# Normalising attention probabilities: one product over four heads instead of two products over two heads each

## The chip, the cores and the metric

The kernel runs on one core of one Trainium2 chip. The metric is the device time of one execution in microseconds. In the profile, PE is TensorE's matmul, PEld its weight load, DVE is VectorE, ACT ScalarE, POOL GpSimd and SP SyncE.

## What is computed

The reference takes x of 8 sequences x 512 tokens x 128 channels and applies three residual steps, each to a layer-normalised input: half of a mixture of experts (8 experts, the best 2 per token, hidden size 512, exact GELU), attention, and half of the same mixture again. The attention has 16 heads of 64 channels, but keys and values are shared by all heads:

```python
q = (x @ Wq).reshape(B, N, h, dh).transpose(0, 2, 1, 3) * scale
kv = x @ Wkv
k, v = (kv[..., :dh], kv[..., dh:])
sim = jnp.einsum('bhid,bjd->bhij', q, k) + bias
sim = jnp.where(causal, -max, sim)
attn = jax.nn.softmax(sim, axis=-1)
out = jnp.einsum('bhij,bjd->bhid', attn, v)
out = out.transpose(0, 2, 1, 3).reshape(B, N, h * dh) @ Wout + bout
```

What matters here is the softmax: each row of exponentials is multiplied by the reciprocal of its sum.

## The kernel before

Everything is in tiles of 128 tokens; there are 32. The kernel has three stages one behind the other: the first mixture of experts (`ffn_*(0)`, 78 expert tiles), attention, and the second mixture (`ffn_*(1)`, 71 expert tiles). Beside the attention, further work of the two mixtures is spread: on POOL the gathers of the first mixture's result (task GA, L757, an indirect DMA for each of two choices of a token tile), on VectorE the combining of it (CB, L1225 and L1230), layer-norm statistics (L974 to L996) and deviations (L1003 to L1007), the scaled rows of the next layer norm (LN, L1243, and X2, L1165), the second routing (H2, L1179 to L1190; W3, L1193 to L1195; B2, L1202 to L1217), and at last the scatter of the rows to their experts (SC, L775, on POOL again).

Attention goes through 8 sequences b, in each through 16 units n = 4g + t: a group g of four heads and a query tile t. Because of the causal mask a unit has (t + 1) x 128 key columns for each head. The steps of one unit are:

- S (TensorE, L1496): scores of four heads in banks.
- TTR (VectorE, L1268), one for each head: adds the bias, writes the negated scores to `prob` and the minimum to `negmax`.
- EXP (ScalarE, L935), one for each head: the exponential in place, with its sum in `lsum`.
- R (VectorE, L1275): the reciprocals of four sums, in `rsum`.
- N (POOL, L785): multiplies `prob` by `rsum`, in place, in two instructions of two heads each.
- T (TensorE, L1505): transposes, four for each key tile; the first waits for N (L1503).
- TC (VectorE, L1281, or ScalarE, L942): copies four transposes from their bank to `pT`.
- AV (TensorE, L1521), O (ScalarE, L948), Y (TensorE, L1528), YA (VectorE, L1290): product with the values, its copy, the output projection and its sum into `x_sb`.

`prob` has 8 buffers, so S of a unit waits for the last T of the unit 8 before. No loop fixes the order in which an engine issues these tasks. A planner (`attention_order`, L453 to L515) runs over a table of tasks, each with a cost in microseconds for the engine that does it and the tasks that it needs (`attention_tasks`, L321); it gives each engine, whenever it is free, that ready task which is wanted earliest (`wanted_at`, L413), and reserves banks as it goes. Its answer, one list for each engine, is the program order. An engine works through its own list strictly in order. The numbers that semaphores are waited for are counted from these lists (`counted`, L521).

The two places that say what a normalisation costs and how it is counted, and the two instructions:

```python
task(("N", b, n), {"pool": (1.25, 2.1, 2.95, 3.8)[t]}, [("R", b, n)])          # L365
NORM, BOUT = counted("pool", ("N",), 2), counted("pool", ("BO",))              # L537
```

Of the kernel before, what the change touches and what calls it, by code (L numbers as in the profile page):

```python
# [9 lines left out]
P = 128  # L10
# [16 lines left out]
HG, NG = 4, 4  # L27
QT = SEQ // P
# [26 lines left out]
ALU = mybir.AluOpType  # L55
# [25 lines left out]
def build(nc, x, Wq, Wkv, Wout, bout, rel_emb, gate_w, fc_w, proj_w, out):  # L81
    ctx = ExitStack()
    with ctx:
# [107 lines left out]
        with att:  # L191
# [11 lines left out]
            prob = [ab(f"prob{n}", [P, HG, (n % QT + 1) * P]) for n in range(8)]  # L203
            negmax = ab("negmax", [P, 8])
            lsum = ab("lsum", [P, 8, HG])
            rsum = ab("rsum", [P, 8, HG])
# [110 lines left out]
        def product_of(t, c):  # L317

            return 0 if t < 2 else c

        def attention_tasks():  # L321
# [3 lines left out]
            def task(name, cost, needs, takes=None, frees=None, banks=1):  # L325
                tasks[name] = (cost, needs, takes and (takes, banks), frees if frees is None or type(frees[0]) is tuple else (frees, 0))

            for b in range(BATCH):
                for q in range(QT):
                    task(("GA", b, q), {"pool": 2.6}, [("CB", b - 1, q // 2)])  # L330
                for z in range(2):
                    opened = [("QL", 0, 0, 1), ("KL", 0)] if b == 1 else []
                    task(("CB", b, z), {"dve": 1.6}, [("GA", b, 2 * z), ("GA", b, 2 * z + 1)] + opened)
                task(("LS", b), {"dve": 2.6}, [("CB", b, 0), ("CB", b, 1), ("LN", b - 1)])
                task(("LA", b), {"act": 3.4}, [("LS", b)])
                task(("LN", b), {"dve": 2.0}, [("xT", b - 1), ("LA", b)])
                task(("BO", b), {"pool": 1.3}, [("LN", b)] + ([("KL", 0)] if b == 0 else []))
                task(("xT", b), {"pe": 0.45}, [("LN", b), ("Q", b - 2, NG - 1, 1), ("V", b - 2), ("K", b - 2)] +
                     ([("N", 0, QT)] if b == 1 else []), "front")
                task(("xTh", b), {"act": 0.48}, [("xT", b), ("Q", b - 2, NG - 1, 1), ("V", b - 2), ("K", b - 2)])  # L340
                task(("xTl", b), {"dve": 0.6}, [("xTh", b)], None, ("xT", b))
                task(("K", b), {"pe": 0.7}, [("xTl", b)] + [("S", b - 2, NU - 1, c) for c in range(2)], "front")
                task(("KH", b), {"act": 0.48}, [("K", b)] + [("S", b - 2, NU - 1, c) for c in range(2)])
                task(("KL", b), {"dve": 0.6}, [("KH", b)], None, ("K", b))
                task(("V", b), {"pe": 1.1}, [("xTl", b), ("AV", b - 2, NU - 1)], "front")
                task(("VC", b), {"act": 0.3}, [("V", b), ("AV", b - 2, NU - 1)], None, ("V", b))
                for g in range(NG):
                    for c in range(2):
                        b2, g2 = (b, g - 2) if g >= 2 else (b - 1, g - 2 + NG)
                        task(("Q", b, g, c), {"pe": 0.7}, [("xTl", b), ("S", b2, g2 * QT + QT - 1, c)], "front")  # L350
                        task(("QH", b, g, c), {"act": 0.5}, [("Q", b, g, c), ("S", b2, g2 * QT + QT - 1, c)])
                        task(("QL", b, g, c), {"dve": 0.6}, [("QH", b, g, c)], None, ("Q", b, g, c))
                for n in range(NU):
                    g, t = divmod(n, QT)
                    for pairs in products(t):
                        task(("S", b, n, pairs[0]), {"pe": (0.68, 0.68, 0.5, 0.66)[t]},
                             [("KL", b), ("T", *earlier(b, n, 8), t)] + [("QL", b, g, c) for c in pairs], "front", None, 2)
                    for h in range(HG):
                        s_task = ("S", b, n, product_of(t, h // 2))
                        others = [("TTR", b, n, h - 2)] if len(products(t)) == 1 and h >= 2 else []  # L360
                        task(("TTR", b, n, h), {"dve": (0.28, 0.41, 0.55, 0.68)[t]}, [s_task, ("EXP", *earlier(b, n, 2), h)] + others,
                             None, (s_task, h % 2) if others or len(products(t)) == 2 else None)
                        task(("EXP", b, n, h), {"act": (0.385, 0.49, 0.6, 0.71)[t]}, [("TTR", b, n, h), ("R", *earlier(b, n, 8))])
                    task(("R", b, n), {"dve": 0.12}, [("EXP", b, n, h) for h in range(HG)] + [("N", *earlier(b, n, 8))])
                    task(("N", b, n), {"pool": (1.25, 2.1, 2.95, 3.8)[t]}, [("R", b, n)])  # L365
                    for jj in range(t + 1):
                        task(("T", b, n, jj), {"pe": 0.44}, [("N", b, n)], "turned")
                        task(("TC", b, n, jj), {"act": 0.48, "dve": 0.6}, [("T", b, n, jj), ("AV", *ring_user(b, n, jj))],
                             None, ("T", b, n, jj))
                    task(("AV", b, n), {"pe": 0.43 * (t + 1) + 0.05}, [("TC", b, n, jj) for jj in range(t + 1)] +  # L370
                         ([("VC", b)] if n == 0 else []) + [("YA", *earlier(b, n, 2))])
                    task(("O", b, n), {"act": 0.36}, [("AV", b, n), ("Y", *earlier(b, n, 2))])
                    task(("Y", b, n), {"pe": 0.45}, [("O", b, n)])
                    task(("YA", b, n), {"dve": 0.25}, [("Y", b, n), ("BO", b)])
                for q in range(QT):
                    task(("ST", b * QT + q), {"dve": 0.25}, [("YA", b, NU - QT + q)])
# [157 lines left out]
        PT_ACT, PT_DVE = counted("act", ("TC",)), counted("dve", ("TC",))  # L534
        MISC_FREE, S_DONE, RSUM = counted("dve", ("xTl", "KL", "QL")), counted("dve", ("TTR",)), counted("dve", ("R",))
        XA_DONE, PROJ_DONE = counted("dve", ("LN",), QT), counted("dve", ("YA",))
        NORM, BOUT = counted("pool", ("N",), 2), counted("pool", ("BO",))  # L537
        YG_DONE = counted("dve", ("CB",), 2)
        XN2_DONE = counted("dve", ("X2",))
        XNT2_PS, XNT2_SB, LOGIT2_PS, LOGIT2_SB = counted("pe", ("T2",)), counted("act", ("C2",)), counted("pe", ("L2",)), counted("dve", ("G2",))  # L540
# [155 lines left out]
        def _(gp):  # L696
            g = nc.gpsimd
# [50 lines left out]
            def attention_pool(tasks):  # L748
                for k in tasks:
                    kind, b = k[0], k[1]  # L750
                    if kind == "GA":
                        q = k[2]
                        t = b * QT + q
                        if b >= 1:
                            gp.wait_ge(yg_done, YG_DONE["CB", b - 1, q // 2])
                        for c in range(TOPK):
                            g.indirect_dma_start(out=yg[:, q, c, :], out_offset=None, in_=y1_dram[t // HT],  # L757
                                                 in_offset=bass.IndirectOffsetOnAxis(ap=pos_row[:, c * TILES + t:c * TILES + t + 1], axis=0),
                                                 ).then_inc(yg_in[q], 16)
                    elif kind == "BO":  # L760

                        gp.wait_ge(xa_done, XA_DONE["LN", b])
                        xb = x_sb[:, b * QT:(b + 1) * QT, :]
                        g.tensor_tensor(out=xb, in0=xb, in1=bout_sb[:].unsqueeze(1).to_broadcast([P, QT, D]),
                                        op=ALU.add).then_inc(bout_done, 1)
                    elif kind == "SC":
                        t = k[1]
                        gp.wait_ge(pos2_done, group_of(t) + 1)
                        gp.wait_ge(id_done, group_of(t) + 1)
                        gp.wait_ge(weights_done, 3 + group_of(t))  # L770
                        if t == 0:
                            gp.wait_ge(fill_done, 16 * FILLS)
                        j = t % (2 * QT)
                        for c in range(TOPK):
                            g.indirect_dma_start(out=slot_dram, in_=slot[:, j, :], in_offset=None,  # L775
                                                 out_offset=bass.IndirectOffsetOnAxis(ap=idx2[:, c, j:j + 1], axis=0),
                                                 ).then_inc(slot_out[half(t)], 16)
                    elif kind == "N":
                        _, _, n = k

                        gp.wait_ge(rsum_done, RSUM["R", b, n])
                        for c in range(2):
                            hs = slice(2 * c, 2 * c + 2)
                            pv = prob[n % 8][:, hs, :]
                            g.tensor_tensor(out=pv, in0=pv, in1=rsum[:, n % 8, hs].unsqueeze(2).to_broadcast([P, 2, (n % QT + 1) * P]),  # L785
                                            op=ALU.mult).then_inc(norm_done, 1)

            def ffn_pool(r):
                k0 = START[r]
# [815 lines left out]
```

## Time and profile before

| | |
|---|---|
| median of 3 runs | 1073.82 us (1072.75 to 1073.89) |
| the profiled execution, its own time | 1075.41 us |
| its span, first to last instruction | 1073.6 us |
| mean granted TensorE clock | 0.962 |
| busy in the span: PE, DVE, ACT, POOL | 950.6, 823.8, 630.6, 621.4 us |
| attention, first normalisation to last projection | 221.6 to about 886 us |

The profiled execution took 1.6 us more than the median of the runs, and 1.8 us more than its span. Busy time says how long an engine had an instruction under way, also one that stood waiting for a shared resource inside itself; a wait for a semaphore counts as idle. A sum over the whole span mixes the three stages, so the attention stage is read by itself below.

### The profile page before, as it was taken

To read this page: it belongs to the slowest core of one execution; us is meant where nothing else is said; L and a number is where in the kernel's file an instruction comes from. 1 tells how busy PE (TensorE), PEld (TensorE's weight loads), DVE (VectorE), ACT (ScalarE), POOL (GpSimd) and SP (SyncE) were. 2 spreads that over 40 slices of the span, in tenths; PEclk is the share of its full clock that TensorE was granted. 3 is DMA by queue.
4 is the path that set the end of the run, shared out by engine and by line. 5 is a ranking of instruction groups with operands and counts; after the bars stand their busy time and mean duration, and the time that the engine had idled before them with its cause. 6 is when DMAs were issued, how large, how long until landed. Compare 5 with 4: busy or idle time off the path is not lost.

```text
span 1073.6 us, 25404 instructions
## 1 busy us (share of the span) xinstructions
PE 950.6 (89%) x7759; PEld 776.1 (72%) x7759; DVE 823.8 (77%) x2972; ACT 630.6 (59%) x1707; POOL 621.4 (58%) x606
## 2 busy tenths in 40 slices
PE   7289998979999998999999889999898881999990
PEld 7289998956666776677776667776676661999990
DVE  6477445478898989997879987779968866777774
ACT  4624334368777777778788667778677662233330
POOL 3656565277766877488554577545485463455551
PEclk9999999989999999999999999999998995999996
DMA  9534552224544652010000000000010003222227
GB/s 273 124 72 104 110 137 74 50 59 94 126 98 105 142 120 56 2 37 7 2 2 2 8 32 4 2 2 2 4 36 4 1 22 107 65 69 70 72 62 235
DMA packets 86498, 69.57 MB, mean 65 GB/s; under 512 B 8018, under 2 KB 76372, under 8 KB 86368
## 3 DMA queue, kind: packets, MB, share of 16 engines
q1 hardware_dynamic: 77104, 48.92, 18.7%
q0 software_dynamic: 9264, 19.03, 6.9%
q8 instruction: 68, 1.11, 0.5%
q14 instruction: 62, 0.51, 0.2%
HBM read 32.07 MB, written 36.31 MB: 64 GB/s over the span
## 4 chain that ended last, share of the span: by engine, by line
PE 64%; DVE 18%; issue 6%; DMA 4%; ACT 3%; POOL 3%; SPq 1%; DVEq 0%; POOLq 0%; ACTq 0%
PE bank L1557 11%; PE bank L1567 11%; PE bank L1496 11%; PE bank L1505 10%; PE bank L1521 9%; PE bank L1528 4%; DVE prob L1268 3%; DVE x_sb L1225 2%; DVE pT L1281 2%; ACT prob L935 2%; PE bank L1383 2%; PE bank L1385 1%; PE bank L1384 1%; PE bank L1549 1%; DMA xr<-xn_dram,gidx 1%
## 5 line engine op out<-in xcount | busy, mean ns | idle before, releaser
L785 POOL TENSOR_TENSOR prob<-prob,rsum 128x256 f32<-128x256 f32 (+3 forms) x256 | 315.0, 1255 | 183.3 <-DVE rsum L1275 182.7
L935 ACT ACTIVATE prob<-prob,negmax 128x384 f32<-128x384 f32 (+3 forms) x512 | 281.8, 552 | 92.7 <-DVE negmax L1268 91.7
L1268 DVE CUSTOM_DVE_ANT_0 prob<-bank,bias_tab 128x384 f32<-128x384 f32 (+3 forms) x512 | 229.3, 484 | 45.0 <-PE bank L1496 42.1
L886 ACT ACTIVATE hT<-bank 128x512 f32<-128x512 f32 x149 | 88.9, 597 | 217.7 <-PE bank L1557 217.7
L1505 PE MATMUL bank<-ident,prob 128*128 128x128 f32 x1280 | 187.8, 280 | 10.2 <-DVE pT L1281 5.0
L1496 PE MATMUL bank<-kst,qst 64*128 64x256 f32 (+2 forms) x1536 | 169.5, 347 | 23.6 <-DVE negmax L1268 16.2
L1505 PEld LDWEIGHTS bank<-ident,prob 128*128 128x128 f32 x1280 | 146.4, 143 | 43.2 <-issue 20.3
L1521 PE MATMUL bank<-pT,vst 128*64 128x256 f32 x1280 | 167.0, 396 | 0.2
L1496 PEld LDWEIGHTS bank<-kst,qst 64*128 64x128 f32 x1536 | 114.5, 190 | 72.8 <-issue 41.1
L1557 PE MATMUL bank<-xrT,w1t 128*128 128x128 f32 x1192 | 162.5, 280 | 3.6 <-DVE xrT L1326 3.4
L1567 PE MATMUL bank<-w_sb,hT 128*128 x1192 | 158.9, 277 | 1.2 <-ACT hT L886 1.2
L1557 PEld LDWEIGHTS bank<-xrT,w1t 128*128 128x128 f32 x1192 | 148.6, 196 | 6.3 <-DVE xrT L1326 5.9
L1567 PEld LDWEIGHTS bank<-w_sb,hT 128*128 128x128 f32 x1192 | 146.5, 194 | 1.5 <-issue 1.4
L1521 PEld LDWEIGHTS bank<-pT,vst 128*64 128x64 f32 x1280 | 83.5, 139 | 54.7 <-issue 22.4
L1281 DVE COPY pT<-bank 128x512 f32<-128x512 f32 x161 | 109.3, 684 | 16.2 <-PE bank L1505 14.2
L798 POOL DMA_INDIRECT xr<-xn_dram,gidx x78 | 78.7, 1009 | 72.6 <-PE bank L1549 65.8
L811 POOL DMA_INDIRECT y_dram<-yo,sidx x71 | 70.0, 986 | 74.7 <-DVE sidx L1324 69.8
L942 ACT ACTIVATE pT<-bank 128x512 f32<-128x512 f32 x159 | 92.6, 588 | 33.9 <-PE bank L1505 33.2
L1338 DVE COPY w1t<-w_sb 128x512 f32 x149 | 64.1, 430 | 59.9 <-PE bank L1557 53.8
L935 ACT ACTIVATION_READ_ACCUMULATOR prob<-prob,negmax 128x1 f32 x512 | 96.6, 189 | 0.0
L1528 PE MATMUL bank<-wo_sb,ot 128*128 128x128 f32 x512 | 83.6, 289 | 3.6 <-ACT ot L948 3.6
L775 POOL DMA_INDIRECT slot_dram<-slot,idx x64 | 62.9, 983 | 37.9 <-DVE idx L1217 21.4
(227 smaller groups left out, 1233.3 us busy)
## 6 DMA issues: line engine op xcount, KB each, us to landing
slot_dram<-fill SPq DMA_DIRECT2D x15, 990.0 KB
y_dram<-yo SPq DMA_DIRECT2D x78, 64.0 KB
xr<-slot_dram SPq DMA_DIRECT2D x71, 66.0 KB, 1.8
w_sb<-L_ffn_fc_w SPq DMA_DIRECT2D x2, 2048.0 KB, 10.0
bias_tab<-bias_dram SPq DMA_DIRECT2D x8, 512.0 KB
slot_dram<-fill SPq DMA_DIRECT2D x2, 1056.0 KB
x_sb<-L_attn_x SPq DMA_DIRECT2D x4, 512.0 KB, 5.7
xn_dram<-xn SPq DMA_DIRECT2D x4, 512.0 KB, 3.2
```

What stands on the lines that cost most here:

```text
L785: g.tensor_tensor(out=pv, in0=pv, in1=rsum[:, n % 8, hs].unsqueeze(2).to_broadcast([P, 2, (n % QT + 1) * P]), op=ALU.mult).then_inc(norm_d ...
L886: a.activation(hT[:, n % 2, :], bank[2 + n % 2][:], ACT.Gelu).then_inc(gelu_done, 1)
L935: a.activation(prob[n % 8][:, h, :], prob[n % 8][:, h, :], ACT.Exp, scale=-1.0, bias=negmax[:, i % 8:i % 8 + 1], accum_out=lsum[:, n % 8, ...
L942: a.activation(pT[:, (b * NB + blk(n, jj)) % RING, :], BANK_OF["T", b, n, jj][:], ACT.Copy).then_inc(pt_act, 1)
L1268: v.tensor_tensor_reduce(out=prob[n % 8][:, h, :], in0=BANK_OF["S", b, n, c0][h % 2][:, at:at + w], in1=bias_tab[:, HG * (n // QT) + h, SE ...
L1281: v.tensor_copy(pT[:, (b * NB + blk(n, jj)) % RING, :], BANK_OF["T", b, n, jj][:]).then_inc(pt_dve, 1)
L1496: ins = t_.matmul(out[o][:, at:at + w], qst[rows, g % 2, zq, c, t * P:(t + 1) * P], kst[rows, b % 2, zk, 0:w], start=(i == 0), stop=(i == 2))
L1505: ins = t_.transpose(out[:, h * P:(h + 1) * P], prob[n % 8][:, h, jj * P:(jj + 1) * P], ident[:])
L1521: ins = t_.matmul(BACK_BANK[n % 2][o * DH:(o + 1) * DH, 0:2 * P], vst[:, b % 2, jj, :], heads, start=(jj == 0), stop=(jj == n % QT))
L1528: ins = t_.matmul(BACK_BANK[n % 2][:, 2 * P:2 * P + D], ot[:, n % 2, c * P:(c + 1) * P], wo_sb[:, n // QT, c, :], start=(c == 0), stop=(c ...
L1557: ins = t_.matmul(bank[2 + n % 2][:, c * P:(c + 1) * P], w1t[:, n % 2, c * P:(c + 1) * P], xrT[:, n % 2, :], start=True, stop=True)
L1567: ins = t_.matmul(bank[6 + n % 2][:, 0:D], hT[:, n % 2, c * P:(c + 1) * P], w2_sb[:, ds(e, 1), c, :].rearrange("p a d -> p (a d)"), start= ...
```

## The change

The two products over two heads become one over four. The planner's cost for the task falls by 0.2 us at each width, and each unit counts once, not twice, on the semaphore `norm_done`.

```diff
-                    task(("N", b, n), {"pool": (1.25, 2.1, 2.95, 3.8)[t]}, [("R", b, n)])
+                    task(("N", b, n), {"pool": (1.05, 1.9, 2.75, 3.6)[t]}, [("R", b, n)])
...
-        NORM, BOUT = counted("pool", ("N",), 2), counted("pool", ("BO",))
+        NORM, BOUT = counted("pool", ("N",)), counted("pool", ("BO",))
...
                         gp.wait_ge(rsum_done, RSUM["R", b, n])
-                        for c in range(2):
-                            hs = slice(2 * c, 2 * c + 2)
-                            pv = prob[n % 8][:, hs, :]
-                            g.tensor_tensor(out=pv, in0=pv, in1=rsum[:, n % 8, hs].unsqueeze(2).to_broadcast([P, 2, (n % QT + 1) * P]),
-                                            op=ALU.mult).then_inc(norm_done, 1)
+                        pv = prob[n % 8][:]
+                        g.tensor_tensor(out=pv, in0=pv, in1=rsum[:, n % 8, :].unsqueeze(2).to_broadcast([P, HG, (n % QT + 1) * P]),
+                                        op=ALU.mult).then_inc(norm_done, 1)
```

Nothing else is edited, but the planner works out the lists of all four engines from these costs.

## Rows read from the trace of the kernel before

**Rows 1.** The page, part 1: busy us, share of the span, instructions.

```profile
PE 950.6 (89%) x7759; PEld 776.1 (72%) x7759; DVE 823.8 (77%) x2972; ACT 630.6 (59%) x1707; POOL 621.4 (58%) x606
```

**Rows 2.** Stretches: length, busy us (instructions) of PE PEld DVE ACT POOL, PEclk, DMA, GB/s.

```profile
221.56:886.20 664.64, 622.03 (x4986) 455.54 (x4986) 566.29 (x1942) 493.45 (x1439) 430.33 (x373) 0.98 0.17 39
...
660.00:740.00 80.00, 79.67 (x668) 59.49 (x666) 62.02 (x225) 64.00 (x188) 40.86 (x34) 1.00 0.01 2
```

**Rows 3.** POOL groups by shape: busy us, mean ns of one, idle before them, releaser.

```profile
L785 POOL TENSOR_TENSOR prob<-prob,rsum 128x1024 f32<-128x1024 f32 x64 | 119.9, 1894 | 67.5 <-DVE rsum L1275 67.4
L785 POOL TENSOR_TENSOR prob<-prob,rsum 128x768 f32<-128x768 f32 x64 | 92.7, 1470 | 40.8 <-DVE rsum L1275 40.5
...
L785 POOL TENSOR_TENSOR prob<-prob,rsum 128x512 f32<-128x512 f32 x64 | 65.3, 1042 | 54.0 <-DVE rsum L1275 53.9
...
L785 POOL TENSOR_TENSOR prob<-prob,rsum 128x256 f32<-128x256 f32 x64 | 38.0, 613 | 21.0 <-DVE rsum L1275 20.9
```

**Rows 4.** TensorE's waits, 221 to 886 us: total us, times, longest.

```profile
PE bank L1496 <- DVE negmax L1268: 16.0, 12, 3.0
PE bank L1505 <- DVE pT L1281: 5.0, 8, 1.2
...
PE bank L1505 <- POOL prob L785: 1.8, 1, 1.8
```

**Rows 5.** The chain that ended last, where attention opens: start us, us, what.

```profile
221.56 1.19 POOL prob L785 x2
...
222.80 0.66 PE bank L1505 x4
```

**Rows 6.** One line's min/median/max ns, then VectorE groups by shape, 221 to 886 us.

```profile
L1225 DVE SCALAR_TENSOR_TENSOR x_sb<-yg,gw,x_sb x32: 318/346/4451, 164.8 to 477.1; 128x128 f32<-128x128 f32 x32
...
L1225 DVE SCALAR_TENSOR_TENSOR x_sb<-yg,gw,x_sb 128x128 f32<-128x128 f32 x28 | 24.9, 931 | 0.1
...
L1165 DVE TENSOR_SCALAR slot<-x_sb,mean,rstd 128x128 f32<-128x128 f32 x30 | 19.5, 670 | 0.0
...
L987 DVE TENSOR_TENSOR lnt<-stats 128x4 f32<-128x4 f32 x8 | 8.7, 1092 | 0.2
L987 DVE TENSOR_TENSOR lnt<-stats 128x8 f32<-128x8 f32 x3 | 6.3, 2105 | 0.0
L989 DVE TENSOR_TENSOR lnt<-stats 128x4 f32<-128x4 f32 x8 | 5.9, 741 | 0.0
...
L988 DVE TENSOR_TENSOR lnt<-stats 128x4 f32<-128x4 f32 x8 | 1.2, 155 | 0.0
```

**Rows 7.** Timelines of VectorE and POOL at five places: start us, us, instruction.

```profile
231.91 4.71 DVE L1225 SCALAR_TENSOR_TENSOR x_sb<-yg,gw,x_sb 128x128 f32<-128x128 f32 x2
...
313.53 3.92 DVE L1225 SCALAR_TENSOR_TENSOR x_sb<-yg,gw,x_sb 128x128 f32<-128x128 f32 x2
...
313.51 3.79 POOL L785 TENSOR_TENSOR prob<-prob,rsum 128x1024 f32<-128x1024 f32 x2 [1.64 <-DVE rsum L1275]
...
600.43 1.08 DVE L1193 TENSOR_SCALAR wt<-wt 128x8 f32<-128x8 f32 x1
...
601.78 1.58 DVE L1195 TENSOR_TENSOR slot<-slot,wt 128x8 f32<-128x8 f32 x1
...
599.59 3.74 POOL L785 TENSOR_TENSOR prob<-prob,rsum 128x1024 f32<-128x1024 f32 x2 [6.19 <-DVE rsum L1275]
...
807.88 4.52 DVE L987 TENSOR_TENSOR lnt<-stats 128x4 f32<-128x4 f32 x1
...
806.65 6.30 POOL L785 TENSOR_TENSOR prob<-prob,rsum 128x768 f32<-128x768 f32 x5
...
861.32 0.74 DVE L1215 TENSOR_TENSOR eqa<-lgb,hot 128x32 f32<-128x32 f32 x1
```

**Rows 8.** Stretches around 814.5 us, columns as in rows 2.

```profile
811.40:814.50 3.10, 0.55 (x6) 0.31 (x3) 2.96 (x12) 0.80 (x2) 1.56 (x3) 1.00 0.00 0
814.50:821.30 6.80, 6.35 (x24) 5.14 (x24) 4.80 (x16) 5.71 (x18) 1.22 (x2) 0.50 0.00 0
```

## The prediction

> **What bounds the kernel now.** I began with the page's busy shares [rows 1]: TensorE leads, VectorE is second, POOL is third with 58%, so a faster POOL is worth something only where somebody waits for it. The change touches the attention stage alone, so I cut that stage out by time [rows 2]: from the first normalisation to the last projection TensorE is busy 622.0 of 664.6 us, VectorE 566.3, POOL 430.3. TensorE is thus idle for 42.6 us of the stage, and a gain has to come out of these (or out of its clock, below). In the stretch from 660 to 740 us, where POOL issues neither gathers nor scatters, TensorE is busy for 79.7 of 80 us: nothing can be won there.
>
> Next, the POOL groups by shape [rows 3]. The 256 products take 315 us, and before them POOL sat idle for 67.5 + 40.8 + 54.0 + 21.0 = 183 us, nearly all of it waiting for the reciprocals. POOL waits for work, not the other way round. The waits of TensorE in the stage [rows 4] say the same: one wait for a product, 1.8 us; 16.0 us of waits for score reductions of VectorE (L1268) and 5.0 us for its copies (L1281). So what TensorE lacks comes late from VectorE. The chain of waits [rows 5] holds a product where the stage opens: the first tile's pair, 1.19 us, and TensorE's transposes behind it.
>
> Last, I looked at why VectorE is late. In its groups [rows 6] one kind of instruction has a mean far above its usual time: the combining products of L1225 have a median of 346 ns and a mean of 931 in the stage, L1165 670, L987 1092 and 2105, L989 741, while L988, the same shape as L987 and right behind it, takes 155. The timelines of both engines beside each other [rows 7] show what holds them: they end some 0.03 to 0.15 us behind a product of POOL. At 313.5 us two of them take 3.92 us together while POOL's pair takes 3.79; at 807.9 us one statistics sum takes 4.52 us, inside a run of five products. Score reductions and copies, which read a bank, I saw nowhere held. I name this **the port hold**: an instruction of VectorE that reads two tiles in SBUF, or scales one, stands while POOL multiplies.
>
> The Trainium skill (SBUF — State Buffer, Who interferes with whom) gives the rule: VectorE and GpSimd share a port pair, and whoever issues first keeps it for the whole instruction. By that rule the trace agrees, as to who is held and until when.
>
> **The change part by part.**
>
> *Removed: half of the products.* The shapes of rows 3 cost 613, 1042, 1470 and 1894 ns for 256, 512, 768 and 1024 columns: 427 ns for each 256 columns, and 186 that an instruction costs whatever its size. The new products have 512, 1024, 1536 and 2048 columns. The first two are in rows 3: 1.04 and 1.89 us. The others are an estimate on the same line: 1894 + 2 x 427 = 2.75 us, and 1894 + 4 x 427 = 3.60. Now a pair takes 3.74 to 3.79 us at the widest and 1.19 at the narrowest [rows 5, 7], since neighbours overlap by some 50 ns. So 0.14 us a tile are saved, 128 x 0.14 = 18 us of POOL. Bounds: 0 (if the columns of a wide product cost more) and 0.19 a tile (no overlap at all).
>
> *What of it is on the path.* At the first tile the full 0.14 us. At the others the product is hidden: TensorE's single further sign of want is the 1.8 us of rows 4, at the same opening, which I count in the 0.14. If this cover were gone, 18 us would be at stake; nothing in rows 4 says so.
>
> *Shorter holds.* Reading through VectorE's timeline I count about 50 tiles whose pair holds one of its instructions until the pair's end, the first at 231.9 and the last at 861.3 us [rows 7]. Each of these ends 0.14 us earlier: 50 x 0.14 = 7.0 us of VectorE. How much reaches TensorE? Against L1225's median, and L988 for the small ones, the held groups of rows 6 lose 28 x 585 + 30 x 324 + 8 x 937 + 3 x 1950 + 8 x 586 ns = 44.2 us, against 16.0 + 5.0 = 21.0 us that TensorE waited for VectorE's reductions and copies: a pass-through of 0.48 at most, since other held lines come on top. I take 0.4: 2.8 us. Bounds 0 and 7.0.
>
> *Lost opening.* Today a second held instruction may slip in between the two products of a tile: at 313.5 us one ends in the middle and the next at the end; at 600.4 and 601.8 us likewise. With one product the first is held to the end and the second runs at once behind it. For two in a row the sum is the same, so the cost is 0; only what stood between them (from 601.51 to 601.78 us: 0.27) moves behind. I count 24 such tiles; the price if it does cost something is the slower rival's. A gain is not excluded by it either, since the second is then free of holds.
>
> *The order.* The planner is told 0.2 us less for each N task (L365) and lays out all four engines' queues anew: gathers and scatters on POOL may stand one place earlier or later against the products, the combining sums on VectorE with them, and so every hold falls elsewhere. The counting of the semaphore (L537) adds no wait: the transposes already waited for both halves (L1503). No row shows the new order. I take 0; bounds by the row nearest to it, a fall of TensorE's clock: at 811.4 us, with VectorE in its long hold, TensorE is busy 0.55 of 3.1 us, and the next 6.8 us are granted 0.50, the 1.2 GHz level [rows 8]; its 6.35 busy us would be half as long at the other level, 2.4 GHz, so that costs 3.2 us. One such event is 2.55 + 3.2 = 5.7 us; less something that the work elsewhere absorbs, 5 us either way.
>
> *Sum.* 0.14 + 2.8 = 2.9 us. The profiled execution takes 1075.41 us (span 1073.6 and 1.8 around it), so 1072.5 for one like it; the median of the runs is 1.6 lower than that execution, hence **1070.9 us**.
>
> **The rivals.**
>
> *A, the forecast:* products shorten, holds shorten with them. 1070.9; own range 1066.7 (7.1 us reach the end) to 1073.7 (only the first tile's).
>
> *B, the longer hold, slower.* A tile's hold loses its opening, and the score reductions queued behind a held instruction on VectorE (in order) wait up to 3.60 us at a stretch, not 1.89 [rows 3, 7]. The second parts are 0.57 to 1.85 us, 1.2 on average; 24 tiles x 1.2 x the pass-through 0.4 = 11.5 us if each costs its whole second part, half of that, 5.7, if every other one does. 1070.9 + 5.7 = 1076.6. It decides when lone held instructions, not pairs of them, meet the first half of a tile. Against it: of the held tiles I counted only two where nothing was held in the second half too. The rule of the Trainium skill named above (SBUF — State Buffer, Who interferes with whom) speaks for this rival: a pair kept for a whole instruction is kept twice as long by one of twice the size.
>
> *C, a luckier order:* the fall of the clock at 814.5, or another, is avoided. 1070.9 - 5 = 1065.9. For it: 42.6 us idle are there to be filled. Against: from 460 us on, with no gathers, little should change.
>
> *D, an unluckier order:* one more such event, 1075.9.
>
> *E, nothing arrives:* wide products cost more per column than narrow ones, or the saving is lost in slack that ends late anyway. 1073.8. Rows 3 are straight to within 5 ns, but end at 1024 columns.
>
> **How the numbers follow.** A measurement of this kernel tells about 0.2% (2.1 us) from no change: faster is below 1071.7, slower above 1076.0. Chances: A 0.38, B 0.18, C 0.17, D 0.13, E 0.14. Of A 0.24 lie below 1071.7 and 0.14 within; with C that is 0.41 faster. B, and most of D, give 0.30 slower. What is left, 0.29, is the same. The range goes from C's 1065.9 to 1078.0, B with a little of its whole price; beyond lie the rest of C, B and D, some 0.2.
>
> **What the profile would show.** Right: 128 products at L785's place of about 1.04, 1.89, 2.75 and 3.60 us, POOL's total in them near 297 us; L1225, L1165 and L987 with means as now or a little less; TensorE's waits for L1268 and L1281 at or below 21 us. For B: holds of over 3 us on VectorE in many more places than the few of now, and those TensorE waits at 26 us or more. For C or D: TensorE's idle time and the stretches at 0.50 change by whole events, at other places than now, and the order of gathers and combining sums differs. For E: products of 1536 and 2048 columns above 2.9 and 3.8 us. The forecast is wrong in kind if TensorE shows new waits for the products themselves, or if the time leaves 1066 to 1078.

## The result and the profile after

| | before | after |
|---|---|---|
| median of the runs | 1073.82 us | 1093.16 us (1088.38 to 1094.41, 3 runs) |
| ratio | | 1.0167, 95% interval 1.013 to 1.0204 |
| span of the profiled execution | 1073.6 us | 1091.3 us |

The change makes the kernel 19 us slower by the medians (18 us by the ratio); 2.9 us less had been forecast. Beside [rows 1] the page of the changed kernel has:

```profile
PE 960.9 (88%) x7759; PEld 782.9 (72%) x7759; DVE 832.8 (76%) x2976; ACT 629.9 (58%) x1703; POOL 603.5 (55%) x478
```

POOL is busy 18 us less, exactly the saving that was worked out, and TensorE is busy 10 us more for the same 7759 matmuls: it ran longer at its lower clock. The groups of the product by shape (columns as in [rows 3]) are those of the estimate, 1.05, 1.90, 2.75 and 3.60 us:

```profile
L783 POOL TENSOR_TENSOR prob<-prob,rsum 128x2048 f32<-128x2048 f32 x32 | 115.3, 3602 | 65.3 <-DVE rsum L1273 65.2
L783 POOL TENSOR_TENSOR prob<-prob,rsum 128x1536 f32<-128x1536 f32 x32 | 88.0, 2751 | 54.3 <-DVE rsum L1273 54.0
...
L783 POOL TENSOR_TENSOR prob<-prob,rsum 128x1024 f32<-128x1024 f32 x32 | 60.7, 1898 | 61.1 <-DVE rsum L1273 61.0
L783 POOL TENSOR_TENSOR prob<-prob,rsum 128x512 f32<-128x512 f32 x32 | 33.5, 1046 | 34.5 <-DVE rsum L1273 34.5
```

The removed lines shift the numbers of all later lines by two: L785 is now L783, L1225 is L1223. So the products did what they should, and the loss lies elsewhere. Where it comes in shows in the timeline of VectorE, whose statistics over eight tiles (L987, now L985) run when sequences 1, 3 and 5 are finished. Before:

```profile
400.04 4.04 DVE L987 TENSOR_TENSOR lnt<-stats 128x8 f32<-128x8 f32 x1
...
560.67 1.14 DVE L987 TENSOR_TENSOR lnt<-stats 128x8 f32<-128x8 f32 x1
...
724.30 1.14 DVE L987 TENSOR_TENSOR lnt<-stats 128x8 f32<-128x8 f32 x1
```

After:

```profile
410.96 0.15 DVE L985 TENSOR_TENSOR lnt<-stats 128x8 f32<-128x8 f32 x1
...
574.35 0.99 DVE L985 TENSOR_TENSOR lnt<-stats 128x8 f32<-128x8 f32 x1
...
741.35 0.99 DVE L985 TENSOR_TENSOR lnt<-stats 128x8 f32<-128x8 f32 x1
```

The first mark starts 11 us later and ends 7 us later (it was held for 4 us before), the second and third come 14 and 17 us later. So the larger part is lost by the second mark, in the first half of the stage. The stage as a whole, beside [rows 2], and one of its holes (length, busy us of PE PEld DVE ACT POOL, PEclk):

```profile
221.56:906.10 684.54, 634.50 (x4989) 464.40 (x4989) 576.15 (x1945) 493.32 (x1435) 412.12 (x245) 0.96 0.17 38
```

```profile
456.00:459.00 3.00, 0.79 (x8) 0.42 (x4) 2.71 (x7) 2.49 (x13) 1.51 (x1) 0.99 0.00 0
459.00:465.80 6.80, 5.60 (x25) 3.54 (x26) 4.53 (x19) 3.70 (x13) 2.93 (x2) 0.50 0.01 2
```

The stage is 19.9 us longer, TensorE idle for 50.0 us of it (42.6 before) and busy for 12.5 us more. The second fence is the pattern of [rows 8] again: after a hole in TensorE's work, 6.8 us at 0.50, the 1.2 GHz level. The stage's mean clock fell from 0.98 to 0.96.

How a hole comes about is best seen at 381 us, in the timelines of VectorE, POOL and TensorE of the changed kernel:

```profile
381.09 3.93 DVE L1223 SCALAR_TENSOR_TENSOR x_sb<-yg,gw,x_sb 128x128 f32<-128x128 f32 x2
...
386.94 0.28 DVE L1288 TENSOR_TENSOR x_sb<-x_sb,bank 128x128 f32<-128x128 f32 x1
...
381.25 3.62 POOL L783 TENSOR_TENSOR prob<-prob,rsum 128x2048 f32<-128x2048 f32 x1 [1.57 <-DVE rsum L1273]
...
387.36 1.97 PE L1519 MATMUL bank<-pT,vst 128*64 128x256 f32 x8 [2.34 <-DVE x_sb L1288]
```

Two combining sums are held for the whole of one product. Behind them in VectorE's list stand more of them, two score reductions and then the sum L1288 that empties a bank; TensorE's product with the values wants that bank, and stands still for 2.34 us. A new kind of wait, L1519 for L1288, leads TensorE's list (total us, times, longest; 221 to 905 us), ahead of the reductions that led in [rows 4]; the kernel before has no such wait in the stage:

```profile
PE bank L1519 <- DVE x_sb L1288: 7.1, 5, 2.8
PE bank L1494 <- DVE negmax L1266: 6.3, 7, 2.2
PE bank L1503 <- DVE pT L1279: 5.2, 6, 1.8
```

### The profile page after: what moved, and what is told of

It is laid out like the page before. It is cut to its first block, busy times and chain, and to the rows that moved or that the text cites. A ratio compares the mean times of both kernels' runs of the same rounds, so it can differ in the third digit from the quotient of the medians.

```text
span 1091.3 us, 25278 instructions
## 1 busy us (share of the span) xinstructions
PE 960.9 (88%) x7759; PEld 782.9 (72%) x7759; DVE 832.8 (76%) x2976; ACT 629.9 (58%) x1703; POOL 603.5 (55%) x478
## 4 chain that ended last, share of the span: by engine, by line
PE 64%; DVE 18%; issue 6%; DMA 5%; POOL 4%; ACT 3%; SPq 1%; DVEq 0%; POOLq 0%; ACTq 0%
PE bank L1555 11%; PE bank L1494 11%; PE bank L1565 11%; PE bank L1503 10%; PE bank L1519 9%; PE bank L1526 4%; DVE x_sb L1223 2%; DVE prob L1266 2%; PE bank L1381 1%; PE bank L1547 1%; DVE pT L1279 1%; DMA xr<-xn_dram,gidx 1%; ACT prob L933 1%; DVE slot L1163 1%; PE bank L1383 1%
## 5 line engine op out<-in xcount | busy, mean ns | idle before, releaser
L783 POOL TENSOR_TENSOR prob<-prob,rsum 128x512 f32<-128x512 f32 (+3 forms) x128 | 296.8, 2324 | 215.2 <-DVE rsum L1273 214.6
L1503 PE MATMUL bank<-ident,prob 128*128 128x128 f32 x1280 | 190.4, 285 | 11.1 <-DVE pT L1279 5.2
L1494 PE MATMUL bank<-kst,qst 64*128 64x256 f32 (+2 forms) x1536 | 173.3, 353 | 16.8 <-DVE negmax L1266 6.6
L1503 PEld LDWEIGHTS bank<-ident,prob 128*128 128x128 f32 x1280 | 149.0, 145 | 45.6 <-issue 21.8
L1519 PE MATMUL bank<-pT,vst 128*64 128x256 f32 x1280 | 167.5, 396 | 7.7 <-DVE x_sb L1288 7.1
L1519 PEld LDWEIGHTS bank<-pT,vst 128*64 128x64 f32 x1280 | 83.6, 138 | 61.2 <-issue 27.9
L1279 DVE COPY pT<-bank 128x512 f32<-128x512 f32 x165 | 111.6, 685 | 17.8 <-PE bank L1503 16.1
L940 ACT ACTIVATE pT<-bank 128x512 f32<-128x512 f32 x155 | 89.9, 589 | 44.7 <-PE bank L1503 44.2
L1526 PEld LDWEIGHTS bank<-wo_sb,ot 128*128 128x128 f32 x512 | 68.2, 194 | 22.7 <-ACT ot L946 11.9
```

The source lines that it names most:

```text
L783: g.tensor_tensor(out=pv, in0=pv, in1=rsum[:, n % 8, :].unsqueeze(2).to_broadcast([P, HG, (n % QT + 1) * P]), op=ALU.mult).then_inc(norm_d ...
L940: a.activation(pT[:, (b * NB + blk(n, jj)) % RING, :], BANK_OF["T", b, n, jj][:], ACT.Copy).then_inc(pt_act, 1)
L1279: v.tensor_copy(pT[:, (b * NB + blk(n, jj)) % RING, :], BANK_OF["T", b, n, jj][:]).then_inc(pt_dve, 1)
L1494: ins = t_.matmul(out[o][:, at:at + w], qst[rows, g % 2, zq, c, t * P:(t + 1) * P], kst[rows, b % 2, zk, 0:w], start=(i == 0), stop=(i == 2))
L1503: ins = t_.transpose(out[:, h * P:(h + 1) * P], prob[n % 8][:, h, jj * P:(jj + 1) * P], ident[:])
L1519: ins = t_.matmul(BACK_BANK[n % 2][o * DH:(o + 1) * DH, 0:2 * P], vst[:, b % 2, jj, :], heads, start=(jj == 0), stop=(jj == n % QT))
```

## The experiments

The change has two parts that an edit can separate: the instructions, and the costs that the planner is told. Two theories: the new order of tasks costs the time, or the longer holds do (rival B). The experiments ran on five chips, and all ratios are to runs of the kernel before on the same chip. On the first two chips that kernel takes 1073 us, on the other three 1103 to 1106 us, so runs of different chips are set beside each other by their ratios only.

### Instructions and order apart

One product, old costs:

```diff
-                    task(("N", b, n), {"pool": (1.05, 1.9, 2.75, 3.6)[t]}, [("R", b, n)])
+                    task(("N", b, n), {"pool": (1.25, 2.1, 2.95, 3.8)[t]}, [("R", b, n)])
```

> One product over four heads, with the planner still told the costs of before, so that all engines issue the tasks in the order of before. The order theory (the lists that the planner worked out anew cost the 19 us, the products themselves gain a little): 1070 to 1073 us, and the blocked instructions of VectorE end 0.14 us earlier. The hold theory (a product of twice the length keeps VectorE's two-tile instructions waiting longer): 1085 us or more with the old order too, VectorE instructions held over 3 us in many more places, TensorE idle more than 43 us in the attention stage.

Measured: 1072.4 us, ratio 1.0004 (0.9987 to 1.0022). The instructions alone do nothing that can be measured. Two products, new costs (the same line the other way, on the kernel before):

> Two products over two heads as before, with the planner told the new, 0.2 us lower costs, so that all engines issue the tasks in the order of the changed kernel. The order theory: 1090 to 1096 us. The hold theory: 1071 to 1077 us. If both share in it, each about half of the 19 us, then about 1083 us.

Measured: 1089.78 us, 1.0149 (1.0101 to 1.0197). The order alone, with not one instruction changed, costs 16 us. The four combinations with a third set of costs, half way between:

```diff
+                    task(("N", b, n), {"pool": (1.15, 2.0, 2.85, 3.7)[t]}, [("R", b, n)])
```

> One product over four heads, the planner told costs half way between (1.15, 2.0, 2.85, 3.7), which gives a third order. The order theory, with the loss due to one particular order: anything from 1066 to 1095 us, and within 3 us of the next run, which has the same order. The hold theory: 1085 to 1095 us.

> Two products over two heads in that same third order. The order theory: within 3 us of the run with one product in this order. The hold theory: some 15 us faster than that run.

| order | two products | one product |
|---|---|---|
| old (costs of before) | 1 | 1.0004 (0.9987 to 1.0022) |
| third (half way) | 1.0065 (1.0035 to 1.0095) | 1.0139 (1.0108 to 1.0171) |
| new (costs of the change) | 1.0149 (1.0101 to 1.0197) | 1.0167 (1.013 to 1.0204) |

So both theories hold something. The order decides, as its theory said; but in the third order the two runs are not within 3 us, one product costs 0.7% more there, which the order theory alone doesn't give. In the new order the two can't be told apart, in the old one there is nothing.

The profiled execution of each shows in what the stage grew. Here it is cut from the first product to the end of the last projection, so that its times are up to 2 us shorter than those above (us):

| | stage | TensorE idle | TensorE busy | VectorE busy |
|---|---|---|---|---|
| two products, old order (before) | 663.6 | 42.0 | 621.6 | 565.4 |
| one product, old order | 661.1 | 41.2 | 619.8 | 564.4 |
| two products, third order | 673.4 | 48.8 | 624.6 | 573.3 |
| one product, third order | 676.6 | 45.2 | 631.4 | 569.6 |
| two products, new order | 679.1 | 53.7 | 625.4 | 578.6 |
| one product, new order (the change) | 682.9 | 49.4 | 633.6 | 575.0 |

With two products the new order adds 11.7 us of idle TensorE and only 3.8 us of slower TensorE. In both slower orders the one long product makes TensorE busy for some 7 to 8 us more (it runs longer at its lower clock) and idle for some 4 us less. The new wait comes with the order, not with the length of the product: it is in the list of two products in the new order too (L1521 and L1290 are the L1519 and L1288 of the changed kernel), and is 1.1 us or less in the third order.

```profile
PE bank L1521 <- DVE x_sb L1290: 8.1, 5, 2.7
```

What a difference of 0.2 us does to the lists shows where TensorE's first differ. Before, and with two products in the new order:

```profile
239.71 1.33 PE L1496 MATMUL bank<-kst,qst 64*128 64x384 f32 x6
240.96 2.83 PE L1521 MATMUL bank<-pT,vst 128*64 128x256 f32 x12
243.72 1.12 PE L1496 MATMUL bank<-kst,qst 64*128 64x384 f32 x6
244.77 0.66 PE L1505 MATMUL bank<-ident,prob 128*128 128x128 f32 x4
```

```profile
239.26 1.33 PE L1496 MATMUL bank<-kst,qst 64*128 64x384 f32 x6
240.52 1.97 PE L1505 MATMUL bank<-ident,prob 128*128 128x128 f32 x8
242.42 1.52 PE L1521 MATMUL bank<-pT,vst 128*64 128x256 f32 x12
243.87 0.79 PE L1496 MATMUL bank<-kst,qst 64*128 64x384 f32 x6
```

A tile's transposes count as ready a moment earlier in the plan, and are put ahead of another tile's product with the values; from there on everything shifts. Four copies of transposes move from ScalarE to VectorE as well (165 there, 161 before). On POOL the gathers, two DMAs for a tile, stand between the products in groups of two to six before, and of two to eight after.

The planner knew a part of this. The time at which its own plan ends, worked out from the kernel's code, is 627.5 us with the old costs, 626.6 with the third and 633.7 with the new ones: it lays out the new order although by its own table that order is 6.2 us longer.

### Which stretch of the order

```diff
-                    task(("N", b, n), {"pool": (1.25, 2.1, 2.95, 3.8)[t]}, [("R", b, n)])
+                    task(("N", b, n), {"pool": ((1.05, 1.9, 2.75, 3.6) if b < 3 else (1.25, 2.1, 2.95, 3.8))[t]}, [("R", b, n)])
```

> One product; the planner is told the new costs for sequences 0 to 2 only (the stretch in which POOL also issues the gathers) and the old ones for 3 to 7. If the loss comes from the early order, as the traces show it arising between 346 and 466 us: 1087 to 1093 us. If it comes from the order over the whole stage, or from the longer products: below 1082 us.

> The reverse: old costs for sequences 0 to 2, new ones for 3 to 7, one product. If the loss comes from the early order: 1072 to 1076 us. Otherwise above 1080 us.

Measured: 1092.5 us, 1.0168 (1.009 to 1.0246), with the new costs in sequences 0 to 2, and 1075.26 us, 1.0019 (1.0 to 1.0038), with them in 3 to 7. The executions of the first kernel scatter (1084.93 to 1101.4 us), but all lie above every one of the kernel before (1076.44 us at most). The loss belongs to the early order, where gathers and combining sums run beside the attention. The new wait of L1521 is in the first kernel's list (6.8 us, 4 times) and not in the second's. Which of its many exchanged tasks does it was not tried.

### Without the port hold

To see what holds are worth, the product was cut to one column of each head, in the old and the new order. It normalises only the first key column and leaves the rest of the probabilities as they are.

```diff
-                        pv = prob[n % 8][:]
+                        pv = prob[n % 8][:, :, 0:1]
...
-                        g.tensor_tensor(out=pv, in0=pv, in1=rsum[:, n % 8, :].unsqueeze(2).to_broadcast([P, HG, (n % QT + 1) * P]),
+                        g.tensor_tensor(out=pv, in0=pv, in1=rsum[:, n % 8, :].unsqueeze(2).to_broadcast([P, HG, 1]),
```

> Order of before; the product normalises only the first key column of each head and leaves out the others (the probabilities stay unnormalised there, so the second mixture routes other rows), so POOL hardly reads and VectorE can hardly be held. If holds are what empties TensorE (some 74 us of held VectorE time, pass-through 0.4): about 30 us faster than before, 1040 to 1048 us. If TensorE lacks work for other reasons: 1062 us or more.

> The same leaving out in the new order. If the new order is bad because it puts held instructions where they hurt (order and holds together), the gap of about 18 us to the old order goes: within 4 us of the run before. If the new order is bad by itself (it makes engines wait for each other whatever the holds), the gap stays: 12 us or more slower than that run.

Measured: old order 1018.62 us, 0.9503 (0.9467 to 0.9539); new order 1023.76 us, 0.9547 (0.9512 to 0.9581). VectorE's groups in the old order, beside [rows 6]: each is back at its free time, or nearly.

```profile
L1165 DVE TENSOR_SCALAR slot<-x_sb,mean,rstd 128x128 f32<-128x128 f32 x32 | 10.1, 337 | 0.0
...
L1225 DVE SCALAR_TENSOR_TENSOR x_sb<-yg,gw,x_sb 128x128 f32<-128x128 f32 x28 | 8.5, 343 | 0.1
L987 DVE TENSOR_TENSOR lnt<-stats 128x4 f32<-128x4 f32 x8 | 1.4, 177 | 0.2
```

And its attention stage, cut like those of the table (columns as in [rows 2]), has TensorE busy for 602.7 of 607.3 us and no fall of the clock:

```profile
219.47:826.81 607.34, 602.74 (x4984) 446.26 (x4985) 496.08 (x1935) 490.43 (x1437) 140.91 (x245) 1.00 0.21 42
```

VectorE does as many instructions as before and is busy for 69 us less: that is all the time for which it was held. Behind the stage both kernels take 188.4 us, so the other routing of the second mixture adds nothing to the gain.

54 us, 5% of the kernel, is more than either theory gave. The order's loss shrinks from about 18 to 5 us. The third order without holds followed on another chip, where the kernel before takes 1105.77 us:

> Without holds (only the first key column of each head is normalised), in the third order, which with one product was 14 us slower than before. If an order's loss comes about through holds: within 3 us of the run without holds in the old order (1018.6). If through the order by itself: 10 us or more above it.

Measured: 1059.74 us, 0.9583 (0.9547 to 0.9619). How far that can be set beside 0.9503 of a faster chip is open, so all three orders ran once more on one chip:

> The kernel without holds (only the first key column of each head is normalised) in the old order, again: 0.95 of before, about 1019 us if this chip runs before in 1073.

> Without holds (only the first key column of each head is normalised), third order, in one call with the old and the new one. The planner's own length of this order is 0.9 us less than that of the old order; if orders lose through holds only, this run is within 2 us of the run in the old order. If the order costs by itself, 6 us or more above it.

> Without holds (only the first key column of each head is normalised), new order. The planner's own length of it is 6.2 us more than that of the old order; if that is the order's loss by itself: 4 to 8 us above the run in the old order, and the remaining 12 or so of the changed kernel's loss come through holds.

| without holds, one chip | us | ratio |
|---|---|---|
| old order | 1061.84 | 0.9607 (0.9571 to 0.9642) |
| third order | 1060.37 | 0.9591 (0.9559 to 0.9623) |
| new order | 1074.91 | 0.9723 (0.9690 to 0.9755) |

The third order, up to 1.4% slower with holds, is as fast as the old one without: its whole loss goes through them. The new order keeps a loss of its own: 0.5% on the faster chip (5 us, near the 6.2 us by which the plan is longer) and 1.2% here (13 us).

These runs also set POOL free, so a control keeps it occupied without reading SBUF: two number sequences into a spare tile, on which the transposes wait.

```diff
...
+                        for done in (filled, norm_done):
+                            fills[0] += 1
+                            gp.wait_ge(filled, fills[0])
+                            g.iota(scratch[:, 0:wide], pattern=[[1, wide]], base=0, channel_multiplier=0,
+                                   allow_small_or_imprecise_dtypes=True).then_inc(done, 1)
```

> Order of before. As the run without holds it normalises only the first key column of each head; then POOL writes two long number sequences to a spare tile that nobody reads, so that POOL is occupied for a time of the order of the product's and the transposes wait for it as before, but without reading SBUF. If the 54 us that the kernel without holds gained came from POOL's reads being out of VectorE's way: 1018 to 1030 us. If they came from POOL being free sooner: 1060 us or more.

Measured: 1075.28 us, 0.9732 (0.9693 to 0.9771), on the chip where the third order without holds has 0.9583; the old order without holds has 0.9607 on the next chip. It lies between the two numbers expected, and VectorE's groups say why (L1175 is L1165 of before, L1235 L1225, L997 L987):

```profile
L1175 DVE TENSOR_SCALAR slot<-x_sb,mean,rstd 128x128 f32<-128x128 f32 x32 | 17.6, 823 | 0.0
...
L1235 DVE SCALAR_TENSOR_TENSOR x_sb<-yg,gw,x_sb 128x128 f32<-128x128 f32 x28 | 8.6, 344 | 3.1 <-DMA yg<-y_dram,pos_row 3.0
...
L997 DVE TENSOR_TENSOR lnt<-stats 128x4 f32<-128x4 f32 x8 | 1.3, 166 | 0.2
```

While POOL only writes, the groups with two inputs are at their free times, but the scaling with one input from SBUF is still held. The Trainium skill (SBUF — State Buffer, Who interferes with whom) distinguishes just these two kinds, and the numbers agree with it. So with POOL busy for as long (the sequences take 307 us), more than half of the gain (2.7 of 3.9%) stays: it came from POOL's reads. The rest is the holds left on L1175 or POOL's time; these runs don't part them.

### Shorter holds

If holds cost so much, many short ones may be better than one long. Four products of one head each, old order:

```diff
...
-                        for c in range(2):
-                            hs = slice(2 * c, 2 * c + 2)
+                        for c in range(HG):
+                            hs = slice(c, c + 1)
...
```

> Order of before, four products of one head each: POOL spends 2 x 0.14 us more on each tile (36 us in all) but no product lasts over 1.04 us. If the length of a single hold matters (the longer-hold theory): 4 to 10 us faster than before. If only the sum of POOL's product time counts, which grows by 12%: 0 to 8 us slower.

Measured: 1096.46 us, 0.992 (0.9892 to 0.9948). Repeated twice:

> Four products of one head each in the old order, again. If shorter holds are really worth it: 0.990 to 0.996 of before. If the 0.992 of the last call belonged to that slower chip: 0.998 to 1.005.

> Four products of one head each in the old order, a third time. 0.990 to 0.996 of before if shorter holds are worth it on any chip; about 1.00 if only on the slower one.

Measured: 0.9905 (0.988 to 0.993) and 0.9923 (0.9891 to 0.9955). These are three different chips, all of the slower kind; on a faster one it was not run. Then the two wider kinds of tiles in eight products of half a head each:

```diff
...
+                        cut = 2 if n % QT >= 2 else 1
+                        w = (n % QT + 1) * P // cut
+                        for i in range(HG * cut):
+                            pv = prob[n % 8][:, i // cut:i // cut + 1, i % cut * w:(i % cut + 1) * w]
...
```

> As that run, but the two wider kinds of tiles (64 of 128) take eight products of half a head. The longest product falls from 1.04 to about 0.6 us, POOL spends some 0.14 x 4 x 64 = 36 us more. If the length of one hold decides: another 2 to 6 us faster than four products. If the sum decides, or POOL becomes late for the transposes: 3 us or more slower than four products.

Measured: 1090.8 us, 0.9875 (0.9835 to 0.9915), the best of all that compute the reference. POOL's products now take 390 us where they took 315, and L1225, here L1226, is held less:

```profile
L786 POOL TENSOR_TENSOR prob<-prob,rsum 128x256 f32<-128x256 f32 x384 | 222.6, 613 | 78.3 <-DVE rsum L1276 77.9
L786 POOL TENSOR_TENSOR prob<-prob,rsum 128x192 f32<-128x192 f32 x256 | 120.5, 505 | 33.2 <-DVE rsum L1276 32.9
L786 POOL TENSOR_TENSOR prob<-prob,rsum 128x128 f32<-128x128 f32 x128 | 47.1, 397 | 11.3 <-DVE rsum L1276 11.1
```

```profile
L1226 DVE SCALAR_TENSOR_TENSOR x_sb<-yg,gw,x_sb 128x128 f32<-128x128 f32 x28 | 21.5, 805 | 2.2 <-DMA yg<-y_dram,pos_row 2.1
L1166 DVE TENSOR_SCALAR slot<-x_sb,mean,rstd 128x128 f32<-128x128 f32 x32 | 13.6, 446 | 0.0
```

In the stage VectorE is busy for 559.5, 553.7 and 560.4 us in the three kernels with four products and for 550.3 us in this one. It was 565.4 before, but on another chip: no trace of the kernel before from these chips is kept.

The opposite of the change is thus the improvement, at the price of more POOL time. Last, a form with one tile as input:

```diff
...
+                        for c in range(HG):
+                            pv = prob[n % 8][:, c, :]
+                            g.tensor_scalar(pv, pv, rsum[:, n % 8, c:c + 1], None, ALU.mult).then_inc(norm_done, 1)
```

> Order of before, each head scaled by its own reciprocal in an instruction with one tile as input and a column of scalars. If POOL does this form faster than 1.67 ns a column, holds shrink with it: at half the time, 74 us of held time become 37 and the kernel takes 1045 to 1055 us. If it does it at the same pace, as the run with four products.

Measured: 1140.26 us, 1.032 (1.0282 to 1.0358). POOL does it slower, not faster, and then TensorE waits for the products themselves:

```profile
L785 POOL TENSOR_SCALAR prob<-prob,rsum 128x512 f32<-128x512 f32 x128 | 198.2, 1563 | 14.7 <-DVE rsum L1275 14.3
...
PE bank L1505 <- POOL prob L785: 59.5, 25, 6.0
```

## Why the prediction was wrong

**What bounds the kernel: right.** TensorE lacks work because VectorE is late, and VectorE is late because of the port hold. The run without holds shows it: 54 us. The control with POOL writing for as long shows that more than half of this came from POOL's reads.

**The product's cost: right.** 0.14 us a tile, 18 us of POOL, none of it on the path ([rows 3, 4]; one product in the old order: 1.0004).

**Shorter holds, 2.8 us: wrong, measured 0.** With one product in the old order VectorE's groups read:

```profile
L1225 DVE SCALAR_TENSOR_TENSOR x_sb<-yg,gw,x_sb 128x128 f32<-128x128 f32 x28 | 24.8, 925 | 0.1
L1165 DVE TENSOR_SCALAR slot<-x_sb,mean,rstd 128x128 f32<-128x128 f32 x32 | 22.1, 711 | 0.0
L987 DVE TENSOR_TENSOR lnt<-stats 128x4 f32<-128x4 f32 x8 | 12.0, 1504 | 0.2
...
L987 DVE TENSOR_TENSOR lnt<-stats 128x8 f32<-128x8 f32 x3 | 5.8, 1941 | 0.0
...
L989 DVE TENSOR_TENSOR lnt<-stats 128x4 f32<-128x4 f32 x8 | 1.2, 152 | 0.0
```

By the working that gave 44.2 us before, with L1225's 346 and L988's 155 as free times, they lose 16.2 + 11.7 + 10.8 + 5.4 + 0 = 44.1 us. L989 is free and L987 ahead of it is held longer by nearly as much: the second hold is merged into the first, as the step "lost opening" put it, and the sum is unchanged. All of VectorE's busy time says the same (564.4 us in the stage, 565.4 before). The 0.14 us a tile is real on POOL, but didn't appear as shorter holds.

**The pass-through of 0.4: too small.** The five groups make 44.1 us (the prediction rounds the sum to 44.2), but all holds together are 69 us. Removing them gave 54 us: about 0.8, with what POOL's shorter work gave included. TensorE's waits that name VectorE's reductions and copies, 21.0 us, are half of its 42.6 us of idle time, and the clock is not in them at all. In the profiled executions the stage's idle time falls by 37 us and TensorE is busy for 19 us less, at a mean clock of 1.00 where it was 0.98.

**The order: the step that failed.** It was put at 0 with 5 us either way; it measured 16 us with the instructions unchanged. The bound was one fall of the clock, as if a new order could spoil one place. But the lists differ from 240 us on, TensorE's and VectorE's at many places, and the delay comes in pieces: of the 15 us that the stage is longer with two products in the new order, only 4 are a slower TensorE. What the step lacked was in reach without a run: the plan that the planner makes of the new costs is itself 6.2 us longer than the old one. The argument "from 460 us on little should change" was wrong for the lists (VectorE's differ until 560 us and beyond) and right for the time (1.0019), and should have made the stretch before it the thing to price: VectorE there is busy for nine tenths of the time and the holds' places matter most.

**Rival B** was named at 0.18 for its mechanism. In the old order it costs nothing, in the new one nothing that can be told, in the third 0.7%; in reverse, with the longest product down from 1.9 to 1.04 and 0.61 us, it is supported: 0.8 to 1.25% faster, though POOL works longer. Of its signs one came and one didn't. Holds of over 3 us on VectorE are 10 in the changed kernel where there were 5, but they are 10 with one product in the old order too, and cost nothing there. TensorE's waits for the reductions and copies are 11.5 us (6.3 + 5.2), not 26. **Rival D**, an unluckier order, is what happened, at three times its price and outside the range. **E** had two reasons. The first is excluded: wide products cost what the line through the narrow ones says. The second, a saving lost in slack, is what one product in the old order shows.

Why this order is bad is shown in part only: most of its loss goes through holds (18 us with them, 5 without, on the faster chips), the rest is its own. Is it the length of the holds or their place? For two products in the new order the five groups, and L1003 beside them, read:

```profile
L1225 DVE SCALAR_TENSOR_TENSOR x_sb<-yg,gw,x_sb 128x128 f32<-128x128 f32 x28 | 31.5, 1160 | 0.6 <-DMA yg<-y_dram,pos_row 0.6
L1165 DVE TENSOR_SCALAR slot<-x_sb,mean,rstd 128x128 f32<-128x128 f32 x32 | 22.8, 739 | 0.0
...
L1003 DVE TENSOR_TENSOR lnt<-lnt 128x4 f32<-128x4 f32 x8 | 7.8, 979 | 0.0
L987 DVE TENSOR_TENSOR lnt<-stats 128x4 f32<-128x4 f32 x8 | 6.8, 850 | 0.2
L989 DVE TENSOR_TENSOR lnt<-stats 128x4 f32<-128x4 f32 x8 | 3.4, 422 | 0.0
L987 DVE TENSOR_TENSOR lnt<-stats 128x8 f32<-128x8 f32 x3 | 2.4, 808 | 0.0
```

Without L1003 that is 22.8 + 12.6 + 5.6 + 2.1 + 2.0 = 45.1 us against 44.1. But the five groups are not all. L1003 takes 7.8 us there; before it was

```profile
L1003 DVE TENSOR_TENSOR lnt<-lnt 128x4 f32<-128x4 f32 x8 | 2.6, 321 | 0.0
```

And all of VectorE is busy for 13.2 us more, of which some 3 are the four copies that it took over. So held time grew by about 10 us in this order. In the third order with one product it grew by less than 3 us (569.6 against 565.4, two copies included), and the kernel still takes 1.4% more. So both count, how long VectorE is held in sum and where. Of the places one kind is seen: the combining sums in front of bank-emptying work, as at 381 us. TensorE waits there for 7 to 8 us in the new order, and not at all in the old one or without holds. For the rest, and for the third order, no place was picked out.

## What to carry to other kernels

Where a program lays out its own order from a table of costs, an edit of a cost is an edit of every engine's list: measure the instruction with the old order first, the order with the old instruction next, compare the length of the planner's own plan, and don't let an honest cost in unless its order was timed. Here three orders whose costs differ by 0.1 us span 1.5%. And where VectorE and POOL work side by side, count the durations above an instruction's own least, over all its groups. Here many short POOL instructions that read SBUF made a faster kernel than few long ones.

## What the runs showed of the hardware

- POOL's product of two inputs is a straight line up to 2048 columns: 1046, 1898, 2751 and 3602 ns at 512, 1024, 1536 and 2048.
- POOL's scaling by a column of scalars (one input tile) takes 1563 ns at 512 columns where the product takes 1042. The Trainium skill (GPSIMD Engine Reference, Engine selection) has GpSimd's one-input elementwise work roughly at line rate and its two-input work about half as fast as VectorE; for this one-input form the measurement says otherwise (it is the slower of the two on POOL), and decides.
- A held VectorE instruction doesn't always get in between two POOL instructions back to back: in [rows 7] one stays for 4.52 us across several of a run of five; at 313.5 us two held ones get in, one behind each product.
- POOL writing alone holds a scaling from SBUF on VectorE (823 ns in the mean, not 337) but not a sum of two tiles (344 ns).
